# Twelve weight units split by VectorE in one fused operation, in place of a scaling on ScalarE and a subtraction on GpSimd

## What is computed

```python
x = x + _L0_gnn_ref(_layernorm(x), adj, W0, b0)          # A @ hidden / deg
# experts: 8 of them, the two best for each row
gate_scores = softmax(xt @ Wg + bg)
topk_scores, topk_idx = top_k(gate_scores, 2)             # renormalised
h = gelu(einsum('td,edf->etf', xt, W1) + b1)
expert_out = einsum('etf,efd->etd', h, W2) + b2
x = x + einsum('te,etd->td', combine, expert_out)
x = x + _L1_gnn_ref(_layernorm(x), adj, W1g, b1g)
```

## Time and profile before

| | |
|---|---|
| median of 3 runs | 1178.93 us (1178.25 to 1179.06) |
| the profiled execution | 1180.73 us, span 1178.9 us |
| TensorE | 986.2 us busy (84%) |
| VectorE | 585.2 us busy (50%) |
| ScalarE | 399.7 us busy (34%) |
| GpSimd | 341.2 us busy (29%) |
| granted TensorE clock | 0.918 of full speed |

### The profile page before, as it was taken

The page is one execution under the profiler, slowest core; times in us unless marked ns, Lnnn a source line. Parts: engine busy times, 40 slices in busy tenths (PEclk is TensorE's granted clock), DMA queues, the critical chain, the costliest instruction groups (busy, mean ns, idle before and its releaser), DMA issues. The chain is left out here.

```text
span 1178.9 us, 23586 instructions
## 1 busy us (share of the span) xinstructions
PE 986.2 (84%) x6868; PEld 641.1 (54%) x6869; DVE 585.2 (50%) x1680; ACT 399.7 (34%) x785; POOL 341.2 (29%) x347
## 2 busy tenths in 40 slices
PE   3679999999613599999999999997199997997941
PEld 1244545444301488888989888896044443453421
DVE  5733212146799556656656656653371116034077
ACT  2572868665653333333333333341120000000000
POOL 3310000003652335445545544544231001001011
PEclk9889999999855699999999999999599998998976
DMA  9576898999782223223223223232799676776301
GB/s 331 185 229 233 279 329 312 325 326 312 263 275 76 73 38 51 46 48 54 45 45 54 50 42 53 50 45 41 237 408 342 232 266 219 239 245 204 114 18 54
DMA packets 86799, 199.96 MB, mean 170 GB/s; under 512 B 12576, under 2 KB 46880, under 8 KB 86624
## 3 DMA queue, kind: packets, MB, share of 16 engines
q1 hardware_dynamic: 65136, 164.70, 40.5%
q0 software_dynamic: 17456, 30.49, 13.2%
q10 hardware_dynamic: 4160, 4.19, 1.1%
HBM read 176.41 MB, written 22.94 MB: 169 GB/s over the span
## 5 line engine op out<-in xcount | busy, mean ns | idle before, releaser
L930 PE MATMUL bank<-adj_f,feat 128*128 128x512 f16 x1024 | 242.4, 391 | 20.3 <-DMA adj_f<-in_adjT 20.3
L1554 PE MATMUL bank<-adj_g,feat 128*128 128x512 f16 x1024 | 242.0, 394 | 14.1 <-DMA adj_g<-in_adjT 14.1
L1151 PE MATMUL bank<-rT,experts 128*128 128x256 f16 x1824 | 209.6, 276 | 3.6 <-DVE rT L1220 3.6
L1172 PE MATMUL bank<-experts,act_h 128*128 x1824 | 205.3, 273 | 1.4 <-DVE y_f L1265 1.4
L1151 PEld LDWEIGHTS bank<-rT,experts 128*128 x1824 | 179.7, 99 | 27.8 <-issue 4.5
L1172 PEld LDWEIGHTS bank<-experts,act_h 128*128 128x128 f16 x1824 | 176.8, 98 | 21.6 <-issue 1.7
L1069 POOL DMA_INDIRECT x_rows<-y,token x76 | 124.5, 1638 | 190.7 <-DVE y L1272 164.1
L1554 PEld LDWEIGHTS bank<-adj_g,feat 128*128 x1024 | 99.4, 97 | 146.5 <-issue 23.8
L930 PEld LDWEIGHTS bank<-adj_f,feat 128*128 128x128 f16 x1024 | 97.4, 97 | 145.6 <-issue 23.6
L1207 ACT ACTIVATE act_f<-bank,b_sb 128x256 f32<-128x256 f32 x304 | 123.7, 475 | 151.3 <-PE bank L1151 151.1
L828 ACT ACTIVATE spent<-adj_f 128x1024 f16<-128x1024 f32 x128 | 135.2, 1056 | 48.8 <-DMA adj_f<-in_adjT 43.0
(11 more groups left out here) (256 smaller groups left out, 894.9 us busy)
## 6 DMA issues: line engine op xcount, KB each, us to landing
adj_f<-in_adjT SPq DMA_DIRECT2D x128, 512.0 KB, 6.1
adj_g<-in_adjT SPq DMA_DIRECT2D x128, 512.0 KB, 5.0
unit_f<-in_W SPq DMA_DIRECT2D x16, 512.0 KB, 7.3
stage<-in_W SPq DMA_DIRECT2D x12, 512.0 KB, 7.1
agg<-in_x ACTq DMA_DIRECT2D x4, 1024.0 KB, 17.1
x_ring<-in_x POOLq DMA_DIRECT2D x4, 1024.0 KB, 11.2
x_rows<-agg SPq DMA_DIRECT2D x4, 1024.0 KB, 10.2
x_sb<-x_rows SPq DMA_DIRECT2D x4, 1024.0 KB, 9.3
```

The costliest lines, as they stand in the source:

```text
L930: last = pe.matmul(mine(s)[ib * DC + c][:, :], feat0[:, j, h, c * P:(c + 1) * P], adj_0[j % RING][:, ib * HALF_SWEEP:(ib + 1) * HALF_SWEEP ...
L1151: last = pe.matmul(pb[2 + q][:, k * SLOT:(k + 1) * SLOT], w1_part(e * DC + (f // FQ * W2_UNIT0 + c), wh)[:, (f % FQ) * P:(f % FQ + 1) * P] ...
L1172: last = pe.matmul(pb[6 + r][:, 0:D], act_h[i][:, ah, f, r * P:(r + 1) * P], experts[:, ds(e * DC + (W2_UNIT0 + f // UH), 1), wh, (f % UH) ...
L1554: last = pe.matmul(mine(s)[ib * DC + c][:, :], feat[:, ds(jg * RING2 + b, 1), h, c * P:(c + 1) * P].rearrange("p a d -> p (a d)"), adj_1[b ...
```

## The change

GpSimd's subtraction and ScalarE's second scaling are taken out. VectorE makes the low part in one operation, 64 times the buffer less the high part. It does this for two units while it waits for the last square root, for two units ahead of its wait for the ranks, and for the other eight behind the tokens. `middle_hi` now counts one for each unit. SyncE's program, ScalarE's wait for all twelve low parts and the late units stay as they are.

```diff
@@ gpsimd
-            def split_middle(u):
-                pool.wait_ge(sem("middle_hi"), 2 * (u - W2_UNIT0) + 2)
-                pool.tensor_tensor(experts[:, u, 1, :], middle_stage(u)[:, :], experts[:, u, 0, :], ALU.subtract
-                                   ).then_inc(sem("middle_lo"), 1)
-
             for n in range(2 * G, 3 * G):
                 low_row(n)
-            for k in range(4):
-                split_middle(W2_UNIT0 + k)
             for n in range(3 * G, NT):
                 low_row(n)
-            for u in range(W2_UNIT0 + 4, LATE_UNIT0):
-                split_middle(u)
@@ vector
+            def split_middle(u):
+                v.wait_ge(sem("middle_hi"), u - W2_UNIT0 + 1)
+                v.scalar_tensor_tensor(out=experts[:, u, 1, :], in0=middle_stage(u)[:, :], scalar=WS, in1=experts[:, u, 0, :],
+                                       op0=ALU.mult, op1=ALU.subtract).then_inc(sem("middle_lo"), 1)
...
-            row_roots(3)
+            row_roots(3, lambda: [split_middle(W2_UNIT0 + k) for k in range(2)])
...
             st.did(v.tensor_copy(count_ps, count_i[:, :]))
+            split_middle(W2_UNIT0 + 2)
+            split_middle(W2_UNIT0 + 3)
             v.wait_ge(sem("ranks_ready"), 1)
...
             st.link(v.tensor_scalar(tokens[:, BLOCKS:BLOCKS + 4 * SR], spare[:, 0:1].broadcast_to([P, 4 * SR]), float(T // 2), None, ALU.add))
+            for u in range(W2_UNIT0 + 4, LATE_UNIT0):
+                split_middle(u)
@@ scalar
                 a.mul(experts[:, u, 0, :], middle_stage(u)[:, :], WS).then_inc(sem("middle_hi"), 1)
-                a.mul(middle_stage(u)[:, :], middle_stage(u)[:, :], WS).then_inc(sem("middle_hi"), 1)
```

## The result

The changed kernel takes 1192.93 us (median of 4, 1191.99 to 1195.12) against 1178.99 (median of 4). The ratio is 1.0122, with a 95% interval of 1.0105 to 1.0140: slower, by 13.9 us. The profiled execution took 1191.99 us with a span of 1189.8. In the second batch of experiments two of the 17 executions of the kernel before took 2683 and 3637 us; they are left out of every figure here.

The account below looks back on a forecast made before the run. VectorE's program sets the routing's end, and a block-end barrier holds the gathers. Tokens come at 2.0 + 2.2 - 6.8 = -2.6 us, but the barrier moves from 384.4 to 397.8: 1178.93 + 13.4 = 1192.3 us, range 1189.0 to 1196.0.

Parts of the forecast that it names:

- the border: End of the first block, at SyncE's first transfer of the next; forecast 0.5 us behind ScalarE's last late unit, at 397.8.
- The collision: In the routing, four f16 one-hots on VectorE slowed beside GpSimd's last four subtractions; removing these saves 6.81 us.
- The first place: Two splits on VectorE in the last norm roots, with only 0.28 us of 2.28 covered by idle time: +2.0 us.
- The second place: Two splits on VectorE ahead of its wait for the ranks, with 0.1 us of cover: +2.2 us.
- From the scan to the one-hots: Routing stretch on VectorE where nothing was to change; ScalarE's removed second scalings were taken as off the path, 0.
- The tail: Behind the tokens: eight VectorE splits, four loads waiting for the fifth split, then ScalarE's late units (3.9 us), ending at 397.3.
- (a): Rival behind the tokens: the loads do not bind, only the eight splits and late units; +10.5, 1189.4 us; chance 4%.
- (b): Rival: collision goes and the work behind the tokens hides under the wait for gathered rows; -2.6, 1176.3 us; chance 3%.
- (c): Rival in the routing: the slow f16 one-hots have another cause and stay; +20.2, 1199.1 us; chance 3%.

Follow-up runs that it names:

- the last four alone: Kernel before with only the last four of twelve splits moved to VectorE, behind the tokens, their second scaling dropped: 1180.24 us against 1180.62, ratio 0.9998.

## Why the prediction was right

It forecast 1192.3 us and +13.4 at the border; 1192.93 was measured, and +13.77. The mechanism was the forecast one, and the 0.37 us between the two sums is what the three terms below were off by (-0.10, +0.31 and +0.16). That the time was hit to 0.6 us is closer than the method can claim, as the four executions of the changed kernel lie between 1191.99 and 1195.12. Its terms, one by one:

**The collision: 6.81 forecast, 6.80 measured** (from the first f16 one-hot to the last instruction of the tokens: 20.08 us before, 13.28 after), and again 6.80 where only the loads moved. This is also the whole of what the change gains.

**The first place: +2.0 forecast, +1.90 measured** (variance to reciprocal, 2.35 us for 0.45). **The second place: +2.2 forecast, +2.51 measured** (reciprocal to scan, 11.74 for 9.23). The difference is the collision that I priced between 0 and 0.7 us and took as 0. GpSimd's last row runs from 337.48 to 338.15 and the third split starts at 337.55:

```profile
337.48 0.67 POOL L439 TENSOR_TENSOR rows_late<-xn,rows_late 128x256 f16<-128x256 f32 x1 [0.27 <-ACT rows_late L852]
```

The two splits take 2.82 us there and 2.35 in the first place, so 0.47 (in each of the four experiments that keep the two splits at this place they take 2.81 us). The value that I took was the wrong end: they overlap by 0.60 us, and nearly all of that was lost. L631's median, on which I leaned, is mostly that of instructions that met nothing. The trace of before had the price all along, one instruction at a time: of the eight between 270 and 281 us, four met one of GpSimd's rows and took 0.67 to 1.07 us, and the other four took 0.47 or 0.48. The dearest and a clean one:

```profile
273.61 1.07 DVE L631 SCALAR_TENSOR_TENSOR agg<-agg,rdeg,x_ring 128x256 f32<-128x256 f32 x1
275.35 0.47 DVE L631 SCALAR_TENSOR_TENSOR agg<-agg,rdeg,x_ring 128x256 f32<-128x256 f32 x1
...
273.71 0.68 POOL L439 TENSOR_TENSOR rows_early<-xn,rows_early 128x256 f16<-128x256 f32 x1
```

The Trainium skill's rule on VectorE instructions with two SBUF inputs (GPSIMD Engine Reference, Key points) holds here; the 0.47 us is its price at this place.

**From the scan to the one-hots, 0 forecast**, 26.94 us before and 26.94 after. ScalarE's scalings were indeed not on the path: with and without them the distance is the same. This stretch also held four of GpSimd's subtractions before, between 338.36 and 348.59, and holds none now, so beside VectorE's work in this stretch, most of which reads PSUM, they cost nothing.

**The tail: forecast 16.0 us more between tokens and border, measured 16.16** (16.83 from the last instruction of the tokens to SyncE's transfer, where it was 0.67). Its inner terms were less exact and made up for each other. The first load landed 3.4 us after its issue and not 4.2; the last one took 5.4 and not 5.0. The border itself cost 0.27 us behind ScalarE (397.07 to 397.34) and not 0.5. By the Trainium skill's formula for a transfer issued by GpSimd (DMA: Bandwidth & Descriptors, Anatomy of one DMA) a lone load was estimated at 3.2 us, and this first load, issued by SyncE, agrees with that to 0.2 us. The four landings are in the changed kernel's group for this tile, from 380 us on:

```profile
DMA to landing us min/median/max: 3.4/5.0/5.4
```

**The rivals.** That the loads do not bind (a) falls with VectorE's waits ahead of its last four splits (1.14, 1.33, 0.24 and 0.20 us, each for a high part that ScalarE makes of a unit just landed), and with the experiment that moved splits 5 to 8: 3.29 us came back. That the tail costs nothing (b) falls twice: with the last four alone the stage is 1.52 us longer where it would have been 6.80 shorter, and moving the late highs across the border gave back 3.66 us. That the slow one-hots have another cause (c) falls with the loads moved first and with the subtractions doubled. The waits of 9.31 and 14.10 us at the border were the row that told (b) from the forecast.

What I had not worked out was that the four slow one-hots could be got rid of without the change. The earlier trace rows had it: the last four loads were issued behind the store of the gates' shares, and nothing in their own conditions held them there.

## What to carry to other kernels

Before work is moved to the engine that sets the end, ask whether the collision that it is to avoid can be avoided in time instead: here one reordering of loads brought 6.8 us, and the move cost 13.8. Work that is put behind the last result of a block is not free because its result is needed later: it holds the border, with everything that its semaphores hold (a ring of buffers, the loads behind it, another engine's last step). Split such a cost in places and check each within one trace; here each measured stage came within half a microsecond of what its experiment expected, where the times of whole executions scatter by two or three.

## What the runs showed of the hardware

An f16 one-hot from SBUF that meets a subtraction on GpSimd does not run at half speed: it lasts until about the end of the subtraction, 2.11 to 2.17 us instead of 0.24 to 0.31 where it stands beside the whole of one, and 1.22 to 1.40 where the subtraction had begun before. Twice as many subtractions stretched twice as many one-hots, eight and not four. The f32 one-hot from PSUM beside the same subtractions stays between 335 and 351 ns. The two forms differ in the type and in the memory of the input at once, and no run here tells which of the two matters. The fused split (f32 and f16 inputs in SBUF, 1.22 us) lost 0.47 us to 0.60 us of overlap with a smaller GpSimd row (0.67 us). And of four 512 KB loads issued from an idle queue 1.14 us apart, the first landed 3.4 us after its issue, the second let ScalarE start 2.55 us after it had started on the first, and the next two followed 1.47 and 1.42 us apart.
